# A language-model layer with a routed feed-forward part: stores of expert outputs on ScalarE's queue, gates computed a pass ahead of their sums, sums split into halves

## What is computed

```
router_probs = softmax(x @ router_w.T + bias)
topk_p, topk_i = top_k(router_probs, 6)
topk_p = topk_p / (sum(topk_p) + 1e-09)            # the gates of a token
# each expert e takes the tokens that chose it (at most C = 768):
hg = expert_in @ w_gate[e].T ; hu = expert_in @ w_up[e].T
expert_out = (silu(hg) * hu) @ w_down[e].T
# each token adds its six expert rows, each times its gate:
sparse[token] = sum_k topk_p[k] * expert_out[row of (token, k)]
out = h + shared_out / 2 + sparse
```

## Time and profile before

| | |
|---|---|
| median of 3 runs | 607.78 us (605.65 to 610.88) |
| profiled execution | 605.81 us, span 604.1 us |
| busy: VectorE, TensorE, GpSimd, ScalarE | 74%, 72%, 67%, 47% of the span |
| granted TensorE clock, mean | 0.847 of full speed |
| DMA, mean over the span | 151 GB/s |

### The profile page before, as it was taken

The page is one execution under the profiler, slowest core; times in us unless marked ns, Lnnn a source line. Parts: engine busy times, 40 slices in busy tenths (PEclk is TensorE's granted clock), DMA queues, the critical chain, the costliest instruction groups (busy, mean ns, idle before and its releaser), DMA issues.

```text
span 604.1 us, 11744 instructions
## 1 busy us (share of the span) xinstructions
PE 433.4 (72%) x2715; PEld 364.1 (60%) x2715; DVE 447.9 (74%) x1686; ACT 284.3 (47%) x806; POOL 404.3 (67%) x426
## 2 busy tenths in 40 slices
PE   2577775755746369989888888988888978697000
PEld 2455654544534259978877777987878978565000
DVE  2678999999997647544445768777878787738998
ACT  2126435524543047767666656556656566242000
POOL 7760067777777777777774777777067777767772
PEclk9999778968985559999898989778988799899555
DMA  7999001111123116777777788887667888433421
GB/s 185 258 242 205 2 37 52 51 50 50 53 86 121 52 69 202 212 222 217 220 208 202 210 229 222 219 228 194 175 185 195 221 214 230 121 83 104 105 68 37
DMA packets 128296, 91.13 MB, mean 151 GB/s; under 512 B 15224, under 2 KB 118245, under 8 KB 127974
## 3 DMA queue, kind: packets, MB, share of 16 engines
q1 hardware_dynamic: 114918, 63.80, 38.7%
q0 software_dynamic: 13312, 26.59, 15.4%
HBM read 46.99 MB, written 44.04 MB: 151 GB/s over the span
## 4 chain that ended last, share of the span: by engine, by line
DVE 41%; PE 33%; SPq 9%; issue 9%; DMA 4%; ACT 4%; POOL 0%; DVEq 0%; ACTq 0%
PE bank L457 9%; DVE emb L924 9%; PE bank L446 8%; SPq L290 6%; DVE gate_junk L914 5%; PE bank L437 5%; PE bank L346 2%; DVE lanes L1012 2%; DMA lanes<-x_rows 2%; DMA emb<-table_dram,idx 2%; DVE hid L1006 2%; ACT hid L626 2%; SPq L297 1%; DVE gate_of L919 1%; SPq L285 1%
## 5 line engine op out<-in xcount | busy, mean ns | idle before, releaser
L1073 POOL DMA_INDIRECT x_rows<-x,to_row x192 | 189.6, 987 | 94.0 <-issue 57.9
L1088 POOL DMA_INDIRECT shared<-o_rows,to_got x192 | 182.6, 951 | 84.0 <-issue 57.3
L457 PE MATMUL bank<-w_down,hid 64*128 x768 | 119.3, 299 | 23.0 <-DVE hid L1006 22.9
L1006 DVE TENSOR_TENSOR hid<-hid,bank 64x512 f32<-64x512 f32 x96 | 66.2, 690 | 86.7 <-ACT hid L626 84.2
L457 PEld LDWEIGHTS bank<-w_down,hid 64*128 64x128 f32 x768 | 100.3, 201 | 37.1 <-issue 29.1
L446 PE MATMUL bank<-x_t,w_now 128*128 128x128 f32 x768 | 114.5, 298 | 0.1
L446 PEld LDWEIGHTS bank<-x_t,w_now 128*128 128x128 f32 x768 | 105.6, 213 | 0.6 <-ACT x_t L621 0.5
L618 ACT ACTIVATE w_now<-w_in 128x128 f32 x384 | 86.3, 297 | 13.7 <-DVE tile_x L794 11.9
L621 ACT ACTIVATE x_t<-bank 128x512 f32<-128x512 f32 x96 | 57.2, 596 | 67.5 <-PE bank L437 65.1
L437 PE MATMUL bank<-ident,lanes 128*128 128x128 f32 x384 | 67.9, 304 | 12.6 <-DMA lanes<-x_rows 11.5
L626 ACT ACTIVATE hid<-bank 64x512 f32<-64x512 f32 x96 | 56.6, 590 | 40.9 <-PE bank L446 40.3
(11 more groups left out here) (210 smaller groups left out, 593.4 us busy)
## 6 DMA issues: line engine op xcount, KB each, us to landing
lanes<-x_rows SPq DMA_DIRECT2D x384, 64.0 KB
o_rows<-lanes SPq DMA_DIRECT2D x96, 256.0 KB
x_rows<-hid_s SPq DMA_DIRECT2D x2, 2048.0 KB, 18.5
x_rows<-x,to_row POOLq DMA_INDIRECT x192, 2.2
shared<-o_rows,to_got POOLq DMA_INDIRECT x192
w_in<-gate_t_dram SPq DMA_DIRECT2D x1, 2048.0 KB
w_in<-up_t_dram SPq DMA_DIRECT2D x1, 2048.0 KB
w_down<-down_t_dram SPq DMA_DIRECT2D x2, 1024.0 KB
```

What stands on the lines that cost most here:

```text
L457: last = pe.matmul(bank_d[k][:, c * P:c * P + P], hid[k][:, c * P:c * P + P], w[:, bass.ds(at[c], P)], start=(c == 0), stop=(c == GROUP - ...
L1006: dve.tensor_tensor(hid[k][:, :], hid[k][:, :], bank_g[k][F:2 * F, :], ALU.mult)\
L1073: pool.indirect_dma_start(x_rows, bass.IndirectOffsetOnAxis(ap=to_row[b][:, t * 8 + j:t * 8 + j + 1], axis=0), x3[b][:, t, :], None, bound ...
L1088: pool.indirect_dma_start(got[n % G_RING][:, j, :], None, o_rows[p], bass.IndirectOffsetOnAxis(ap=to_got[b][:, t * 8 + j:t * 8 + j + 1], a ...
```

## The change

Three things:

1. **Stores.** SP only loads; nothing stands between its loads. `act_store` issues store `q - 3` on ScalarE's queue, in ScalarE's step `q`, behind silu of `q - 1` and before the weights of `q + 1`; its wait for the copy is ScalarE's now. The last two stores go out in the first two rounds of the shared experts.
2. **Gates.** `dve_gates` does the six picks and the scaling for a token, into a `gate_of` that holds all 32 tokens. `GATES_IN` says how many tokens' gates fall into each pass: 16, 6, 10. In pass 0 they stand in steps 2, 4, 6, ..., 32, in pass 1 in steps 34, 39, 45, 51, 56, 62, in pass 2 in ten steps from 68 to 93. The gates need the fetch of their sequence, so all eight fetches now stand in steps 1 to 8 (before: steps 2 to 4, 36 to 38, 70 and 71).
3. **Sums.** `dve_sums` does three of a token's six sums after one step and three after the next. The first token is in steps 45 and 46, and a token follows each 2.9 steps. `FIRST_LATE` becomes 18, so 14 tokens are late; behind the loop both halves follow each other. Steps 45, 51, 70, 73, 84, 87 and 90 carry gates and a half of sums.

```diff
--- before.py
+++ after.py
@@ -50,9 +50,11 @@
 STEP0 = [sum(STEPS_OF[:p]) for p in range(len(PASSES))]
 STEPS = sum(STEPS_OF)
 X_RING, O_RING, G_RING = 6, 4, 8
-LOAD_LEAD, STORE_LAG = 3, 3
-
-STEPS_PER_TOKENS = 3.0
+STORE_LAG = 3
+
+FETCH_STEP, STEPS_PER_TOKENS = 43.0, 2.9
+
+GATES_IN = (16, 6, 10)
 
 
 
@@ -185,7 +187,7 @@
         row_x = sb("row_x", [P, 2])
         gate_junk = sb("gate_junk", [P, TOP, EXPERTS])
         tile_junk = gate_junk[:, 0:4, :]
-        gate_of = [sb(f"gate_of{k}", [P, 8]) for k in range(2)]
+        gate_of = sb("gate_of", [P, BATCHES * TILES, 8])
         gate_raw = [sb(f"gate_raw{k}", [P, 8]) for k in range(2)]
 
 
@@ -234,13 +236,19 @@
         TOKENS = [(b, t) for b in range(BATCHES) for t in range(TILES)]
 
 
-        TOKENS_AT, at = {}, 0.0
+        SUM_AT, at = {}, FETCH_STEP
         for n, (b, t) in enumerate(TOKENS):
             p = PASS_OF[b]
             at = max(at, STEP0[p] + STEPS_OF[p] + 3.0) + STEPS_PER_TOKENS
-            TOKENS_AT.setdefault(int(at) + 1, []).append(n)
-        FETCH_AT = {STEP0[PASS_OF[b]] + 2 + b - FIRST[PASS_OF[b]]: b for b in range(BATCHES)}
-        FIRST_LATE = min(n for step, ns in TOKENS_AT.items() if step >= STEPS + 2 for n in ns)
+            SUM_AT[int(at)] = (n, 0)
+            SUM_AT[int(at) + 1] = (n, 1)
+        FETCH_AT = {1 + b: b for b in range(BATCHES)}
+        GATES_AT = {}
+        for p, some in enumerate(GATES_IN):
+            first, steps = (2, STEPS_OF[p] - 2) if p == 0 else (STEP0[p], STEPS_OF[p])
+            for k in range(some):
+                GATES_AT[first + k * steps // some] = sum(GATES_IN[:p]) + k
+        FIRST_LATE = min(n for step, (n, half) in SUM_AT.items() if step + 1 - half >= STEPS + 2)
         LATE_SEQS = list(range(FIRST_LATE // TILES, BATCHES))[::-1]
         SHARED_ORDER = LATE_SEQS + [b for b in range(BATCHES) if b not in LATE_SEQS]
 
@@ -290,18 +298,8 @@
                     sp.dma_start(x_in[q % X_RING][:, c, :], x_rows[bass.ds(at[c], P), :])\
                         .then_inc(sem(f"x_in{q % X_RING}"), 16)
 
-            def store(q):
-                p = max(k for k in range(len(PASSES)) if STEP0[k] <= q)
-                i = q - STEP0[p]
-                sp.wait_ge(sem("o_out"), q + 1)
-                sp.dma_start(o_rows[p][i * SEQ:(i + 1) * SEQ, :].rearrange("(c r) d -> r c d", r=P),
-                             quarter(o_out[q % O_RING])).then_inc(sem(f"stored{q % O_RING}"), 16)
-
-            for q in range(-LOAD_LEAD, STEPS + STORE_LAG):
-                if q + LOAD_LEAD < STEPS:
-                    load(q + LOAD_LEAD)
-                if q >= STORE_LAG:
-                    store(q - STORE_LAG)
+            for q in range(STEPS):
+                load(q)
             for k, b in enumerate(SHARED_ORDER):
                 if (b + 1) * TILES <= FIRST_LATE:
                     sp.wait_ge(sem("shared_add"), k + 1)
@@ -598,6 +596,13 @@
                 act.wait_ge(sem("router_logits"), b + 1)
                 act.activation(prob[b][:, :, 2:], rl[:, :, :], ACT.Exp).then_inc(sem("prob"), 1)
 
+        def act_store(act, q):
+            p = max(k for k in range(len(PASSES)) if STEP0[k] <= q)
+            i = q - STEP0[p]
+            act.wait_ge(sem("o_out"), q + 1)
+            act.dma_start(o_rows[p][i * SEQ:(i + 1) * SEQ, :].rearrange("(c r) d -> r c d", r=P),
+                          quarter(o_out[q % O_RING])).then_inc(sem(f"stored{q % O_RING}"), 16)
+
         @block.scalar
         def _(act):
             act.wait_ge(sem("rows"), 16)
@@ -624,12 +629,16 @@
                     act.wait_ge(sem("pe_in"), q)
                     wait(act, "pe_down", q - 2)
                     act.activation(hid[k][:, :], bank_g[k][0:F, :], ACT.Silu).then_inc(sem("silu"), 1)
+                if q >= STORE_LAG:
+                    act_store(act, q - STORE_LAG)
             for n in range(BATCHES + 1):
                 if n < BATCHES:
                     act.wait_ge(sem("pe_x_t"), STEPS + n + 1)
                     act.wait_ge(sem("pe_in"), STEPS)
                     wait(act, "pe_si", 2 * n - 2)
                     act.activation(x_t[n % 2][:, :], bank_x[n % 2][:, :], ACT.Copy).then_inc(sem("x_t"), 1)
+                if n + 1 < STORE_LAG:
+                    act_store(act, STEPS + n + 1 - STORE_LAG)
                 if n >= 1:
                     k = (n - 1) % 2
                     act.wait_ge(sem("pe_si"), 2 * n - 1)
@@ -905,27 +914,31 @@
             dve.tensor_scalar(to_got[b][:, :], top_place[b][:, :, :].rearrange("p t k -> p (t k)"), -1.0,
                               float(TILES_OF[p] * P), ALU.mult, ALU.min).then_inc(sem("to_got"), 1)
 
-        def dve_token(dve, n):
-
+        def dve_gates(dve, n):
 
             b, t = TOKENS[n]
-            k = n % 2
+            dve.wait_ge(sem("fetch"), 2 * b + 2)
             for j in range(TOP):
                 last = dve.scalar_tensor_tensor(gate_junk[:, j, :], place[b][:, t, :], top_place[b][:, t, j:j + 1],
                                                 prob[b][:, t, 2:], ALU.is_equal, ALU.mult,
-                                                accum_out=gate_raw[k][:, j:j + 1])
-            last.then_inc(sem("gate"), 1)
-            dve.wait_ge(sem("gate"), 2 * n + 1)
-            dve.tensor_scalar(gate_of[k][:, 0:TOP], gate_raw[k][:, 0:TOP], top_inv[b][:, t:t + 1], None, ALU.mult)\
+                                                accum_out=gate_raw[n % 2][:, j:j + 1])
+            last.then_inc(sem("gate_raw"), 1)
+            dve.wait_ge(sem("gate_raw"), n + 1)
+            dve.tensor_scalar(gate_of[:, n, 0:TOP], gate_raw[n % 2][:, 0:TOP], top_inv[b][:, t:t + 1], None, ALU.mult)\
                .then_inc(sem("gate"), 1)
-            dve.wait_ge(sem("gate"), 2 * n + 2)
-            dve.wait_ge(sem(f"got{n % G_RING}"), 16 * TOP * (n // G_RING + 1))
-            for j in range(TOP):
-                dve.scalar_tensor_tensor(emb[b][:, t, :], got[n % G_RING][:, j, :], gate_of[k][:, j:j + 1],
+
+        def dve_sums(dve, n, half):
+
+            b, t = TOKENS[n]
+            if half == 0:
+                dve.wait_ge(sem("gate"), n + 1)
+                dve.wait_ge(sem(f"got{n % G_RING}"), 16 * TOP * (n // G_RING + 1))
+            for j in range(half * TOP // 2, (half + 1) * TOP // 2):
+                if j:
+                    dve.wait_ge(sem("summed"), (TOP - 1) * n + j)
+                dve.scalar_tensor_tensor(emb[b][:, t, :], got[n % G_RING][:, j, :], gate_of[:, n, j:j + 1],
                                          emb[b][:, t, :], ALU.mult, ALU.add)\
                    .then_inc(sem("summed" if j < TOP - 1 else "token_done"), 1)
-                if j < TOP - 1:
-                    dve.wait_ge(sem("summed"), (TOP - 1) * n + j + 1)
 
         @block.vector
         def _(dve):
@@ -1012,9 +1025,10 @@
                     dve.tensor_copy(o_out[s], bank_d[(q - 2) % 2][:, :]).then_inc(sem("o_out"), 1)
                 if q in FETCH_AT:
                     dve_fetch(dve, FETCH_AT[q])
-                for n in TOKENS_AT.get(q, []):
-                    if n < FIRST_LATE:
-                        dve_token(dve, n)
+                if q in GATES_AT:
+                    dve_gates(dve, GATES_AT[q])
+                if q in SUM_AT and SUM_AT[q][0] < FIRST_LATE:
+                    dve_sums(dve, *SUM_AT[q])
             late = FIRST_LATE
             for n in range(BATCHES + 1):
                 if n < BATCHES:
@@ -1035,10 +1049,12 @@
                 if n >= len(LATE_SEQS) and n % 2 == 1:
                     dve.wait_ge(sem("shared_add"), len(LATE_SEQS))
                     if late < len(TOKENS):
-                        dve_token(dve, late)
+                        dve_sums(dve, late, 0)
+                        dve_sums(dve, late, 1)
                         late += 1
             for n in range(late, len(TOKENS)):
-                dve_token(dve, n)
+                dve_sums(dve, n, 0)
+                dve_sums(dve, n, 1)
 
 
         @block.gpsimd
```

## The result

The changed kernel takes **575.84 us** (median of 4 runs, 574.52 to 577.37) against 609.09 for the kernel before on the same chip (4 runs, 605.65 to 610.88): a ratio of 0.9461, interval [0.9406, 0.9517]. The forecast was 577, its range 573 to 596. The profiled execution took 577.37 with a span of 575.6 (the first to the last instruction), where the forecast's span was 573.2.

What follows compares the result with a forecast made beforehand. It took GpSimd's gather chain, started by finishing passes, plus VectorE's lag as the bound. Last gather at 566.7, then 2.2 landing, 2.3 sum and 2.0 gave span 573.2; 3.7 more gave 577 us, range 573 to 596.

Steps and rivals of the forecast that it cites:

- the end is GpSimd's chain of gathers: Whole kernel before: gathers that start when passes finish set its end, plus VectorE's lag; removing waits and lag gives 30.9 us.
- GpSimd's floor: GpSimd from scatters through 192 gathers without stops, 1.253 us each: last gather starts at 566.7, span ends at 573.2.
- The end behind the last gather: Tail after the last gather starts: landing 2.2, sum 2.3, 2.0 to the span's end, about 6.5 us.
- Deadlines of the copies: Passes 0 to 2: copies 33, 67 and 95 must start by 322.7, 412.9 and 503.1; expected 317.2, 405.6, near 480.
- the overload of the first steps: Pass 0, steps 2 to 8: fetches and gates cost VectorE 24.7 us against TensorE's 18.0; 5.6 charged.
- the clock at 1.00 in passes 1 and 2: Sign that the forecast is right: TensorE's granted clock stays at 1.00 in passes 1 and 2.
- The 4.3 us from a copy to its gather: From a pass's last copy to its first gather: copy 0.69, wait for ScalarE's `hid` 0.53, store to gather 3.1.
- six steps of lead: SP's queue: loads may run six steps ahead, some 15 us, which covers a step of about 2.6 us with long issues.
- the lower bound: ScalarE's step: the store's issue runs beside `hid`, 2.42 us a step, under TensorE's 2.57, so it costs nothing.
- rival of 3.01 a step: ScalarE becomes the bound: the store's issue waits until `hid` ends, 3.01 us a step, 595 us; chance 0.13.
- rival of excluding issues: The two queues' issues exclude each other, so SP's step stays at 3.12 us and the time is 600; chance 0.09.
- slower rival: VectorE bursts delay copies, the store's wait stops ScalarE, TensorE idles and its clock falls: 632 us; chance 0.05.

## Why the prediction was right

**The number: close, and partly by luck.** The forecast of 577 lies 1.2 us over the median of 575.84. Its span was 2.4 us too short (573.2 against 575.6). On that I put 1.7 from the span to the profiled execution, which holds (577.37 - 575.6), and 2.0 more to the median, as before; here the median lies 1.5 under the profiled execution. The two errors run against each other.

**What ended the kernel before: misread.** I wrote that "the end is GpSimd's chain of gathers" and saw VectorE as a lag behind it. The chain that ended last held no gather then; it was the loop and VectorE's late tokens, with GpSimd's chain some 4 us under it. The forecast didn't suffer, because the change takes away both: copy 95 comes 42 us earlier and the tail's gates are gone, so that GpSimd's chain, which hardly changes, is left as the end. It did mislead the expectation of the stores alone.

**GpSimd's floor: right.** First gather at 328.02 (predicted 326.98), gather 73 at 418.38 (417.2), 145 at 508.57 (507.4), the last at 567.88 (566.7). The distances are exact to 0.2 us; all are 1.0 to 1.2 late because this execution's scatters start 1.2 later, 80.17 against 78.93. The experiments bear it out from both sides: an earlier loop gives nothing (spread fetches), fewer gathers give 37.5 us.

**The end behind the last gather: mis-sized.** I put 2.2 + 2.3 + 2.0 = 6.5; it is 7.8. The term at fault is the landing, for which I took the scatters' row: VectorE's sums start 3.4 us behind the last gather's issue (567.88 to 571.31). With the front's 1.2 that is the 2.4 by which 573.2 missed 575.6.

**Deadlines of the copies.** The distance from copy 33 to copy 67 is 88.0 where I had 88.4, and the overload of the first steps 90.5 - 33 x 2.57 = 5.7 (from the first copy, 229.93, to copy 33, 320.43) where I charged 5.6. With the fetches spread, the same distance is 84.9, so the overload is the crowded first steps. But the first copy itself was 3.1 late, so that copy 33 came at 320.43 and not 317.2, copy 67 at 408.41 and not 405.6. 1.2 of the 3.1 is the later front; the rest is open. It isn't the fetch that now stands ahead of this copy: the stores-alone kernel has none there, and its first copy comes at 229.97. Copy 95 came at 486.3 instead of near 480: 2.8 is copy 67's, and pass 2 took 77.9 us where 28 steps of 2.57 are 72.0. Here I had priced nothing. Six of its steps carry gates and a half of sums (70, 73, 84, 87, 90 and 93; the list of the change leaves out the last), and in each the copies are 3.97 to 4.1 us apart. In one of them (step 84) TensorE stands for 1.26 us, and from 455.2 on the granted clock is 0.50 for 6.8 us, which makes the average 0.91 from 449 to 486. So the sign "the clock at 1.00 in passes 1 and 2" held in pass 1 alone. It is harmless, because gather 145 comes at 508.57. The 4.3 us from a copy to its gather was short too: 414.52, the store's issue with three buffers, to 419.16 alone are 4.6, and from the copy it is 5.5. So the margin at copy 67 is not 7 us but 418.4 - 5.5 - 408.4 = 4.5.

**SP: the right direction, too small a term.** I put 2.4 us a step, 2.6 with long issues. Undisturbed steps take that (359.80 - 357.37 = 2.42 between the first instructions of two steps), but the mean is 2.72: long issues add 0.19 a step in that stretch, and register loads slower than their usual 0.30 another 0.09. My sentence that six steps of lead cover it decided more than it claimed: with three buffers the same SP has copy 67 start 5.3 us later, 8.5 counted from the first copy.

**ScalarE: the lower bound.** The issue runs beside `hid`, as the register loads had, with 0.35 more until `w_now`; pass 1 with 34 of them is at 2.59 a step. The rival of 3.01 a step is refuted by that, and the rival of excluding issues by SP: the median of its load issues stays 333 ns with ScalarE issuing stores beside it. The Trainium skill (Perfetto Trace Analysis, DMA Instruction — HWDGE (DVE, Sync)) has one generator locked by one sequencer at a time; nothing here shows SP held by it: its four issues of a step take 1.53 us with the long ones, 1.50 before. The slower rival's mechanism exists but is small: `w_now` waits for the copy of a store in 12 steps, 18.7 us together in the list of waits (us in total, times, longest):

```profile
ACT w_now L623 <- DVE lanes L1025: 18.7, 12, 2.3
```

In the stores-alone kernel, with whole tokens on VectorE, it is 46.9 us in 16 steps, up to 8.1.

The Trainium skill's other rule, that a second issuing queue saves sequencer time only and that this is usually small (DMA: Bandwidth & Descriptors, Issuing engines are not separate DMA queues), agrees with the trace in its first half: what left SP is the 0.43 us of the store's issue and its wait. In its second half the measurement decides otherwise for this kernel, where the sequencer was the bound of pass 0: the move alone gave 0.8%, 2.5% with token 0 later, and some 28 us on top of the gates and sums.

**Part 3, the halves,** I had as what keeps the pieces under 1.1 us and the clock up. With the sums whole, 2.3 us after one step, TensorE is idle for 4.0 us of pass 1 (314.7 to 406.4) and the clock is 1.00 all the same; nothing of it reaches the end (576.21). I gave the split no price of its own, and it has none.

**The parts don't add.** Gates and sums alone give 1.0%, the stores alone 0.8% (2.5% with a later token), all together 5.4%. In the loop, SP's 3.14 a step and VectorE's 3.3 lie side by side, so that each part uncovers the other's limit. At the end, two more lie 4 us apart: with whole tokens the span ends 75 to 77 us behind copy 95 whatever GpSimd does, so a part pays only by what it moves copy 95; and close below that stands GpSimd's chain, which gives back only its own stops.

## What to carry to other kernels

Look for an engine's idle time by what ends it, not for a full engine: GpSimd is 70% busy and sets the end of the kernel after. Then follow the chain back from the last instruction before you call an engine's stops the price: before the change, GpSimd's three stops were real, and the end hung on another chain that was 4 us longer. Where two limits lie within 6% of each other, price the parts of a change together, and ask of each new speed what it will now reach too early. A queue that is slower than the loop by 0.15 us a step can be hidden by a lead, but count how many steps the lead pays for.

## What the runs showed of the hardware

- A gather of 128 rows of 512 bytes by GpSimd costs it 0.94 to 1.06 us (median 0.945) and 0.30 until the next starts: 192 of them in 239.5 to 240.1 us from the first start to the last, in the kernel after and in every variant of it where GpSimd didn't have to stop, with copy 67 anywhere from 403.8 to 411.2 beside it. Its rows can be used 2.8 (570.45 - 567.61, five rows awaited) to 3.4 us behind the issue; a scatter's landing is given as 2.2.
- ScalarE issues a 256 KB store while its own ACTIVATE runs: the issue starts 0.01 us behind `hid` and takes 0.37 (357.58); the next ACTIVATE starts 0.84 behind `hid`'s start instead of 0.49.
- With rows of 512 bytes the 16 DMA engines held 251 GB/s at a share of 0.91 for 88 us, next to 210 at 0.77 in the earlier trace rows, and TensorE waited for no load in that execution. The prediction's 257 at 0.94 was close.
- SP's issues of 64 KB loads have a median of 333 ns, but 17 of 384 in either kernel are over 0.6 us, up to 1.6 before and 1.9 after; what the issues take over their median is 0.16 and 0.18 us a step on average, and an estimate from medians misses it.
